# Attention and feed-forward layer: statistics, root and normalisation of the coming inputs moved by two head pairs

## The reference, cut to what matters

```
xn = (x - mean(x)) / sqrt(var(x) + 1e-5)              # per token
q, k, v = xn Wq / 8, xn Wk, xn Wv                      # per head
o = softmax(q k^T) v
x = x + o Wp + bp
x = x + ffn((x - mean(x)) / sqrt(var(x) + 1e-5))       # LN, ternary 128 -> 512, gelu, LN, ternary 512 -> 128
```

## Time and profile before

| | us |
|---|---|
| median of 3 runs | 1171.57 (1168.80 to 1172.42) |
| the profiled execution, its own time | 1170.42 |
| its span, first to last instruction | 1168.6 |
| TensorE busy | 1054.0 (90%) |
| ScalarE busy | 957.2 (82%) |
| VectorE busy | 920.3 (79%) |
| GpSimd busy | 918.1 (79%) |
| mean granted TensorE clock | 0.964 of full speed |

### The profile page before, as it was taken

The page is one execution under the profiler, slowest core; times in us unless marked ns, Lnnn a source line. Parts: engine busy times, 40 slices in busy tenths (PEclk is TensorE's granted clock), DMA queues, the critical chain, the costliest instruction groups (busy, mean ns, idle before and its releaser), DMA issues.

```text
span 1168.6 us, 40480 instructions
## 1 busy us (share of the span) xinstructions
PE 1054.0 (90%) x16160; PEld 816.9 (70%) x16160; DVE 920.3 (79%) x1989; ACT 957.2 (82%) x1322; POOL 918.1 (79%) x874
## 2 busy tenths in 40 slices
PE   3688999998999999999999999999999999969998
PEld 1466777776777777777777777777777777757777
DVE  5689878887777777777777777777777778669998
ACT  2587888887888888888888888888888889959998
POOL 2367888887888888888888888888888888967775
PEclk9999999999999999999999999999999999989999
DMA  9111122122211121222112121222222212221111
GB/s 210 38 15 25 38 38 39 38 38 35 42 30 28 38 39 38 39 39 38 38 38 25 34 38 38 38 38 38 38 38 34 42 25 40 51 38 38 29 38 47
DMA packets 159785, 47.56 MB, mean 41 GB/s; under 512 B 141168, under 2 KB 159344, under 8 KB 159600
## 3 DMA queue, kind: packets, MB, share of 16 engines
q1 hardware_dynamic: 159600, 44.97, 21.4%
HBM read 7.21 MB, written 4.19 MB: 10 GB/s over the span
## 4 chain that ended last, share of the span: by engine, by line
PE 52%; ACT 15%; POOL 14%; issue 13%; DVE 3%; DMA 1%; ACTq 0%; SPq 0%; POOLq 0%; DVEq 0%
PE S L471 11%; POOL pl L805 7%; PE S L463 5%; PE PV L490 5%; POOL xn L789 4%; ACT p L669 4%; PE PV L492 3%; PE PV L491 3%; PE M L444 3%; PE QK L431 3%; PE QK L432 3%; PE QK L433 3%; ACT ph L677 3%; ACT zTh L750 3%; ACT z L737 2%
## 5 line engine op out<-in xcount | busy, mean ns | idle before, releaser
L805 POOL TENSOR_TENSOR pl<-p,ph 128x1024 f16<-128x1024 f32 x256 | 546.7, 2136 | 163.9 <-ACT ph L677 157.5
L669 ACT ACTIVATE p<-S,s_exp 128x1024 f32<-128x1024 f32 x256 | 285.0, 1113 | 96.0 <-PE S L471 96.0
L943 DVE TENSOR_REDUCE negmax<-M 128x4 f32<-128x1024 f32 x256 | 311.4, 1216 | 59.9 <-PE M L444 59.8
L677 ACT ACTIVATE ph<-p 128x1024 f16<-128x1024 f32 x256 | 270.5, 1057 | 8.2
L971 DVE TENSOR_TENSOR QKl<-QK,QKh 128x512 f16<-128x512 f32 x256 | 176.2, 688 | 100.8 <-ACT QKh L685 100.4
L490 PEld LDWEIGHTS PV<-V,ph 128*128 128x128 f16 x2048 | 187.1, 99 | 67.0 <-issue 63.4
L490 PE MATMUL PV<-V,ph 128*128 128x65 f16 x2048 | 219.0, 195 | 10.3 <-DVE O L965 10.2
L491 PE MATMUL PV<-V,ph 128*128 128x64 f16 x2048 | 216.8, 194 | 0.0
L492 PE MATMUL PV<-V,pl 128*128 128x65 f16 x2048 | 215.8, 195 | 0.0
L492 PEld LDWEIGHTS PV<-V,pl 128*128 128x128 f16 x2048 | 190.8, 98 | 0.0
L491 PEld LDWEIGHTS PV<-V,ph 128*128 128x128 f16 x2048 | 190.7, 98 | 0.0
(11 more groups left out here) (145 smaller groups left out, 2499.9 us busy)
## 6 DMA issues: line engine op xcount, KB each, us to landing
result<-X SPq DMA_DIRECT2D x16, 256.0 KB, 2.3
X<-in_L_attn_query SPq DMA_DIRECT2D x7, 512.0 KB, 7.1
OT<-O SPq DMA_TRANSPOSE x64, 4.5
O<-in_L_attn_Wq SPq DMA_DIRECT2D x1, 512.0 KB, 4.9
O<-in_L_attn_Wk SPq DMA_DIRECT2D x1, 512.0 KB, 6.7
X<-in_L_attn_query SPq DMA_DIRECT2D x2, 256.0 KB, 5.4
O<-in_L_attn_Wv SPq DMA_DIRECT2D x1, 512.0 KB, 6.0
w<-in_L_ffn_w SPq DMA_DIRECT2D x2, 256.0 KB, 5.1
```

The costliest lines, as they stand in the source:

```text
L669: e.activation(p32[r][:, :, :, :].rearrange("p i m n -> p (i m n)"), S[:, :], ACT.Exp, scale=s_exp[:, :]).then_inc(s_ex, 1)
L677: e.activation(ph[r][:, :, :, :].rearrange("p i m n -> p (i m n)"), p32[r][:, :, :, :].rearrange("p i m n -> p (i m n)"), ACT.Copy).then_i ...
L805: e.tensor_tensor(pl[r][:, :, :, :].rearrange("p i m n -> p (i m n)"), p32[r][:, :, :, :].rearrange("p i m n -> p (i m n)"), ph[r][:, :, : ...
L943: e.tensor_reduce(negmax[g % 2][:, :].rearrange("p (i c) -> p i c", i=2)[:, :, NB * jj:NB * jj + NB], M[:, :].rearrange("p (i t m) -> p i ...
```

## The change

Statistics and root move from pair 2 to pair 0 of a batch, normalisation and the addition of bp from pair 3 to pair 1. The transposes stay at pair 4. For batch 1 (b = -1) this is from steps -6 and -5 to -8 and -7. Batches 2 to 31 follow with b = 0 to 29; batch 30 and 31 of the loop have no such work.

```
 def x_stats_batch(b, j):
 
-    return b + 2 if j == 2 and 1 <= b + 2 < B else None
+    return b + 2 if j == 0 and 1 <= b + 2 < B else None
 
 
 def x_norm_batch(b, j):
-    return b + 2 if j == 3 and 1 <= b + 2 < B else None
+    return b + 2 if j == 1 and 1 <= b + 2 < B else None
```

## The result

Faster: 1081.64 us (1080.79 to 1085.65, 4 runs) against 1171.28 (1168.80 to 1172.42, 4 runs). The ratio is 0.9244, with an interval of 0.9216 to 0.9272. The forecast was 1078, with a range of 1069 to 1097.

The account below looks back on a forecast made before the run. TensorE, 90% busy, was taken as the bound, held up by its wait for xn and the slow clock behind it. Savings of 73.7 (steady batches), 5.6 (prologue) and 13.2 (batches 0 to 7) make 92.5 off 1170.42: 1078 us, range 1069 to 1097.

Parts of the forecast that it names:

- The bound and the wait: Batches 8 to 29: TensorE waits 2.08 us a batch for xn, 45.7 us in all; the change removes it.
- The clock: Batches 8 to 29: half clock follows the idle gap; without the gap the clock stays 1.00, saving 28.0 us.
- Rival C: The half clock is not the gap's doing, so only waits are saved: 61.5 us, 1109 us; chance 0.04.
- The steady batch, 27.40: Each of batches 8 to 29 takes 27.40 us, batch 12's busy time; 73.7 us saved over 22 batches.
- the second way: Check of the steady batch: batch 30's 26.99 us plus the transposes' 0.43 is 27.42.
- Cover on VectorE: Pair 1: statistics delay O and qk_low, leaving 0.37 and 0.43 us before TensorE reads them, so nothing waits.
- GpSimd's delay: Pairs 0 and 1: GpSimd falls back about 2 us, but TensorE reads p_low's output late enough; caught up later.
- The prologue: Before batch 0: the transposes' wait of 6.35 us goes, early statistics lose 0.67 to 0.75; net -5.6 us.
- Batches 0 to 7: Batches where weights are prepared, 248.83 us before: 13.2 us saved in sum.
- my own test for being wrong: Wrong if a steady batch takes over 28 us, or batches 0 to 7 with prologue gain under 10 of 18.8.
- statistics move 0.67 from behind one weight step to ahead of another: Batches 1 and 2: some TensorE waits for O rise, some fall; net -0.9 us, bounds -3 and +2.
- upper bound for batch 7: VectorE's lbrep step may wait out one more p_low: up to 3.5 us lost, where 1.0 was taken.

Follow-up runs that it names:

- The run with xn alone: Kernel before with normalisation and the addition of bp in pair 2 instead of pair 3, statistics and root left in pair 2: 1086.35 us, ratio 0.927.
- the run without it: Kernel before with statistics and root in pair 0, normalisation and bp left in pair 3: 1123.36 us in one profiled run.
- the filled gap: Kernel before with 18 unread matmuls of 256 columns ahead of TensorE's wait for xn, from batch 2 on: 1145.32 us, ratio 0.9774.
- the weight steps first: Changed kernel with VectorE's weight steps ahead of the statistics in each step instead of behind them: 1075.53 us, ratio 0.9186.
- the run with four more: Changed kernel with four more unread bn_stats ahead of the statistics in pair 0 of the loop's batches 8 to 29: 1096.94 us.

## Why the prediction was right, and where it was not

- **The bound and the wait.** Right. TensorE's only wait in the steady batches was xn's lateness of 2.08 us, and two pairs put xn 4.58 ahead (forecast 4.6). The run with xn alone shows that one pair does it; the run without it shows that statistics and root do not.
- **The clock.** Right: 28.0 us were given to it, and the filled gap gave 29.2 with the wait kept. Rival C is out. The Trainium skill's page TensorE: Matmul & The Clock Gate (Why this matters for your kernels), cited there, warns only of idle gaps longer than this one; here the half clock did follow gaps of 2.08, and went when they were filled.
- **The steady batch, 27.40.** 0.19 us too high, 4.2 us in all. The step "busy time of batch 12" took TensorE's busy 27.40 as the work, and the second way added the transposes' 0.43 to batch 30. Behind an idle gap they are busy for 0.41 us and more; in a full stream they take 0.22. Batch 30 plus 0.22 is 27.21. The forecast had this only as the lower edge of its range.
- **Cover on VectorE.** Right: no wait came; 0.26 to 0.32 us by experiment against 0.37. GpSimd's delay covered, as forecast.
- **The prologue.** Right, 5.4 for 5.6.
- **Batches 0 to 7.** This is the term that was mis-sized: 13.2 us forecast, 5.6 measured, and my own test for being wrong asked for at least 10 of 18.8 with the prologue, where 11.0 came. The step that failed is "statistics move 0.67 from behind one weight step to ahead of another", with batch 4 counted as a plain gain of 2.08. The order was priced by the statistics' own length. What it really changes is whether VectorE's instruction starts ahead of or behind `p_low`: 1.6 us more for L1009 and 1.8 for L1034, with the half clock behind them. Batch 4 lost 1.7 instead of gaining 2.1, which is half of the shortfall. Batch 1 lost 2.0, but batch 2 gained 2.4, by the same mechanism with its sign turned (L1031), so for these two together the forecast of 0.9 came near (0.4). The second part of the shortfall has another cause: batch 6 gained 0.6 for a forecast of 2.5, since L1045 took 3.5 us more. The forecast had taken 1.0 off for the weight steps in that gap, but had not asked whether their length would change: when L1045 starts, at 236.54, GpSimd now runs two `p_low` one behind the other (235.56 to 239.78). Batch 7 gained 0.1 for 1.1: the wait for lbrep grew by 0.6 and a stretch of half clock came behind it. The row that would have told was the earlier trace rows: L1050 and L1034 are one shape with two durations. I used it as an upper bound for batch 7 alone, and should have asked of every weight step what GpSimd is doing when it starts.
- **The sum** came out near partly by luck: the errors, +4.2 in the steady batches, -7.6 in batches 0 to 7, -0.2 in the prologue and +0.7 in the tail, have nothing to do with each other and partly cancel.

What stays open: which batches of 0 to 7 get a stretch of half clock varies from kernel to kernel even where nothing was changed (3.6 us in one case, 5.0 in another), and no run here tells why. The length of the gap alone does not decide it. In batch 6 of the changed kernel a gap of 2.95 us ends at 241.86 and the clock stays up; with the weight steps first nearly the same gap, 2.94, ends at 234.91 and the clock is down. Of each, a microsecond just behind:

```profile
242.00:243.00 1.00, 1.00 (x28) 0.96 (x26) 1.00 (x3) 0.97 (x2) 0.00 (x0) 1.00 0.95 185
```

```profile
235.00:236.00 1.00, 1.00 (x21) 1.00 (x21) 1.00 (x3) 0.97 (x2) 0.00 (x0) 0.50 0.91 177
```

## What to carry to other kernels

An engine that is busy 90% of the time can be freed by moving work of engines that are busy 80%: look for the one wait of the busiest engine, and put its producer ahead by as many steps as it takes, with the distance read from the timeline. One step was enough here, and the rest of the move paid only in the prologue. After any reordering, compare the duration of every VectorE instruction against the same line and shape before. If it grew, look at what GpSimd was doing when it started: here a swap with its neighbour gave the time back for L1009 and L1034, a move by a pair did for L1050, and for L1045 it did so only in part.

## What the runs showed of the hardware

- A gap of 2.08 us in TensorE's stream was followed by a stretch at 1.2 GHz in 18 of 22 batches, and that cost 1.5 us, three quarters of the gap again. Gaps of 1.2, 1.42 and 1.67 us, one in each of the 22 batches, were followed by none. In the weight batches gaps of up to 2.95 were followed by none as well, and one of 1.96 by a stretch, so these lengths are no limits. Two thirds of a microsecond less waiting was worth 1.9 us a batch.
- A VectorE `tensor_scalar` of four columns took 2.04 us or 0.16, by whether it started 0.12 us behind or 0.57 ahead of a GpSimd instruction of 2.12. Two `bn_stats` that started 0.21 us behind such an instruction (484.62 and 484.41 in the run with four more) kept their 0.24 us each.
- The two transposes moved TensorE's next instruction on by 0.22 us in a full stream, where the timeline gives them 0.38; behind a gap they were busy for 0.41.
